# A graph layer with residual norm on one core: ScalarE issues the stores of the output and the loads of x_t, x and adj; SyncE's queue keeps the hops over HBM

## The reference: what is computed

```
u     = h h^T / sqrt(384);  p = softmax(u);  delta = p * adjacency
attn  = delta / (sum(delta over keys) + 1e-10)
ctx   = upper(attn) (h W_left^T + b_left) + diag(attn) (h W_self^T + b_self)
      + lower(attn) (h W_right^T + b_right)
o     = relu(layernorm(ctx, 1e-12) * gamma + beta)
out   = layernorm(h + o, 1e-5)
```

## Time and profile before

| | us |
|---|---|
| median of 3 runs | 458.61 |
| the profiled execution, whole | 459.64 |
| its span, first to last instruction | 457.9 |
| TensorE busy in it | 448.1 |
| VectorE busy | 386.6 |
| ScalarE busy | 323.9 |
| GpSimd busy | 209.6 |

### The profile page before, as it was taken

How to read it: one execution, slowest core, us unless ns; L and a number is a source line. 1 busy time by engine, 2 the same in 40 slices (tenths; PEclk the granted TensorE clock), 3 DMA queues, 4 the chain that set the end, 5 groups by cost and what they waited for, 6 DMA issues and landing times.

```text
span 457.9 us, 9725 instructions
## 1 busy us (share of the span) xinstructions
PE 448.1 (98%) x2636; PEld 445.3 (97%) x2636; DVE 386.6 (84%) x1366; ACT 323.9 (71%) x716; POOL 209.6 (46%) x295
## 2 busy tenths in 40 slices
PE   8999999999999999999999999999999999999993
PEld 7999999999999999999999999999999999998992
DVE  6877988888898887989878989888988888887876
ACT  6756677677678677678677678677677677676764
POOL 1144346553345553345554345553345553345542
PEclk9999999999999999999999999999999999999998
DMA  8765455666455565455566555566455666444312
GB/s 265 219 212 178 130 175 185 194 203 196 131 179 195 189 205 185 145 176 196 181 195 190 158 174 191 181 214 195 143 168 181 188 215 189 152 159 142 108 59 104
DMA packets 84227, 80.60 MB, mean 176 GB/s; under 512 B 7148, under 2 KB 76528, under 8 KB 84208
## 3 DMA queue, kind: packets, MB, share of 16 engines
q1 hardware_dynamic: 84000, 80.24, 55.0%
q10 hardware_dynamic: 144, 0.13, 0.1%
q0 software_dynamic: 64, 0.01, 0.0%
HBM read 52.04 MB, written 28.31 MB: 175 GB/s over the span
## 4 chain that ended last, share of the span: by engine, by line
PE 91%; DVE 2%; DMA 2%; ACT 1%; issue 1%; SPq 1%; POOL 1%; POOLq 0%; DVEq 0%; ACTq 0%
PE ps_proj L508 60%; PE ps_ctx L542 20%; PE ps_scores L485 3%; PE ps_scores L479 2%; PE ps_scores L481 2%; PE ps_proj L493 1%; PE ps_scores L431 1%; DMA cross_raw<-cross_dram 1%; DMA rows<-in_L_gnn_b_right 1%; PE ps_ctx L536 0%; ACT ps_scores L606 0%; SPq L332 0%; DVE delta L829 0%; POOL rstd L1138 0%; PE ps_ctx L538 0%
## 5 line engine op out<-in xcount | busy, mean ns | idle before, releaser
L508 PE MATMUL ps_proj<-w_hi,xt_split 128*128 128x384 f32 x1128 | 236.0, 334 | 0.0
L508 PEld LDWEIGHTS ps_proj<-w_hi,xt_split 128*128 128x128 f32 x1128 | 199.1, 188 | 0.0
L508 PE MATMUL ps_proj<-w_lo,xt_split 128*128 128x384 f32 x564 | 128.0, 334 | 0.0
L1138 POOL TENSOR_TENSOR rstd<-var_eps,minus_half 128x4 f32<-128x4 f32 x31 | 34.4, 1110 | 186.5 <-DVE var_eps L890 186.5
L508 PEld LDWEIGHTS ps_proj<-w_lo,xt_split 128*128 128x128 f32 x564 | 100.5, 188 | 0.0
L624 ACT ACTIVATE ps_proj<-bias 128x384 f32<-128x384 f32 x188 | 90.4, 494 | 2.0 <-DVE proj_lo L860 1.8
L1144 POOL TENSOR_TENSOR scaled<-normed,gamma_sb 128x384 f32<-128x384 f32 x60 | 61.7, 1029 | 30.9 <-ACT normed L654 30.9
L628 ACT ACTIVATE proj_hi<-ps_proj 128x384 fp32r<-128x384 f32 x128 | 63.4, 496 | 15.2 <-PE ps_proj L508 14.4
L648 ACT ACTIVATE ps_ctx<-ps_proj,diag 128x384 f32<-128x384 f32 x64 | 35.5, 555 | 49.2 <-PE ps_proj L508 49.2
L860 DVE TENSOR_TENSOR proj_lo<-ps_proj,proj_hi 128x384 fp32r<-128x384 f32 x128 | 67.3, 544 | 1.4 <-ACT proj_hi L628 1.4
L1148 POOL TENSOR_TENSOR shifted<-scaled,beta_sb 128x384 f32<-128x384 f32 x61 | 62.4, 1024 | 2.5
(11 more groups left out here) (113 smaller groups left out, 676.3 us busy)
## 6 DMA issues: line engine op xcount, KB each, us to landing
x_sb<-in_x SPq DMA_DIRECT2D x32, 384.0 KB, 4.3
xt_sb<-in_x_t SPq DMA_DIRECT2D x31, 384.0 KB, 3.8
out_dram<-out_sb SPq DMA_DIRECT2D x31, 384.0 KB, 2.9
adj_sb<-in_adj SPq DMA_DIRECT2D x32, 256.0 KB, 4.4
dt_dram<-turned SPq DMA_DIRECT2D x31, 256.0 KB, 2.0
dt_raw<-dt_dram SPq DMA_DIRECT2D x124, 64.0 KB, 2.0
cross_dram<-cross_turned SPq DMA_DIRECT2D x29, 256.0 KB, 2.0
cross_raw<-cross_dram SPq DMA_DIRECT2D x116, 64.0 KB, 2.0
```

The lines of the kernel that those rows point to most:

```text
L508: mm = nc.tensor.matmul(ps_proj[bank(at, g)][:, 0:H], halves[c][half], moving[w][:, c, :], start=False, stop=True, skip_group_check=True)
```

## The change

From the second batch on, SyncE's stream holds only the two hops. ScalarE's stream gets, in each batch b: the load of x_t of batch b + 4 behind the last `split_proj`, the load of x of batch b + 2 behind `split_xt`, the load of adj of batch b + 2 behind the last seed of the next batch, and behind it the store of the output of batch b - 2. So x_t is loaded for the batch b + 4 in place of b + 3, and the output is stored in the batch in which it is written and not in the one after. Each keeps a wait in front of it. The first batch's issues stay on SyncE, as do the last three output stores.

```
--- before.py
+++ after.py
-            def load(b, slot):
-                sp.dma_start(x_sb[slot][:], x_rows[b]).then_inc(x_loaded[slot], 16)
-                sp.dma_start(adj_sb[slot][:], adj_rows[b]).then_inc(adj_loaded[slot], 16)
...
             def one(at):
                 nxt, ahead, third = at.plus(1), at.plus(2), at.plus(3)
-                if at.plus(-3).exists(BATCHES):
-                    store(at.plus(-3))
-                if third.exists(BATCHES):
-                    if at.plus(-1).exists(BATCHES):
-                        sp.wait_ge(xt_lo_ready, at.n(1, C - 1))
+                if at.b == 0:
                     load_xt(third.n(1), third.slot(UNROLL))
-                if at.b == 0:
...
-                if ahead.exists(BATCHES):
-                    if at.plus(-2).exists(BATCHES):
-
-                        sp.wait_ge(y_ready, at.n(T, -T))
-                    load(ahead.n(1), ahead.slot(UNROLL))
                 if nxt.exists(BATCHES):
                     store_turned(nxt)
...
+            def store(at):
+                act.wait_ge(out_ready, at.n(T, T))
+                act.dma_start(out_rows[at.n(1)], out_sb[at.slot(2)][:]).then_inc(stored[at.slot(2)], 16)
+
+            def load_xt(at):
+
+                fourth = at.plus(4)
+                if fourth.exists(BATCHES):
+                    act.wait_ge(xt_lo_ready, at.n(1, C))
+                    act.dma_start(xt_sb[fourth.slot(UNROLL)][:], xt_rows[fourth.n(1)]).then_inc(xt_loaded[fourth.slot(UNROLL)], 16)
+
+            def load_x(at):
+                ahead = at.plus(2)
+                if ahead.exists(BATCHES):
+                    if at.plus(-2).exists(BATCHES):
+
+                        act.wait_ge(y_ready, at.n(T, -T))
+                    act.dma_start(x_sb[ahead.slot(UNROLL)][:], x_rows[ahead.n(1)]).then_inc(x_loaded[ahead.slot(UNROLL)], 16)
+
+            def load_adj(at):
+                ahead = at.plus(2)
+                if ahead.exists(BATCHES):
+
+                    act.wait_ge(delta_ready, at.n(T * T, 0))
+                    act.dma_start(adj_sb[ahead.slot(UNROLL)][:], adj_rows[ahead.n(1)]).then_inc(adj_loaded[ahead.slot(UNROLL)], 16)
...
@@ -700,6 +712,7 @@
                 if at.b == 0:
 
+                    load_xt(at)
                     return
...
                 split_proj(at, 3)
+                load_xt(at)
                 seed_ctx(at, 0)
...
                     split_xt(third)
+                load_x(at)
                 seed_ctx(at, 1)
...
                     seed_proj(nxt, 3)
+                load_adj(at)
+                if second.exists(BATCHES):
+                    store(second)
```

## The result

The changed kernel takes 498.86 us (median of 5 runs, 497.68 to 500.0) against 458.65 (458.46 to 460.08) for the kernel before, run beside it: a ratio of 1.0874, interval 1.0863 to 1.0886. It is 40 us slower. The forecast was 458.9 and no change; the range ended at 463.0. The profiled execution took 500.0 us with a span of 498.3, where before's took 459.64 with 457.9.

What follows compares the result with a forecast made beforehand. TensorE, gapless in 30 of 31 batches, was taken as the bound. Terms 0 + 0 + 0.3 = +0.3 us on the profiled 459.64 gave 459.9, in the median 458.9; the range was 457.4 to 463.0.

Steps and rivals of the forecast that it cites:

- What bounds the kernel, and that SyncE's time is worth nothing: TensorE runs without a gap in 30 of 31 batches, 13.71 us each; freeing SyncE shortens nothing.
- Part 1: Four more issues on ScalarE, 0.61 us each, 2.4 us a batch, fit its idle places; cost 0.
- the lower bound: ScalarE's issues cost nothing at all if each runs beside the activation before it; upper bound 1.46 us, the longest issue.
- Part 2: What moved transfers run beside: adj and output, issued amid the `cross_raw` loads, delay them within reserve; steady-batch cost 0.
- I count nothing: The load of x may hold up the store to `cross_dram`; the `dt_raw` loads stand before `cross_raw`, so 0 was counted.
- D: Added delay of `cross_raw` from bulk beside it: bounds 0 and 1.84 us, taken 0.5, against reserves of 0.44 and 1.18.
- Part 1's cover of `dt_full`: `dt_full` comes 0.2 us later in one batch, on average not; delay passes at most in full to L812 and `delta`.
- Part 2's rule weighed, taking turns: DMA engines alternate packets between loaded queues, so ScalarE's bulk takes every second turn beside the hop; no trace row showed it.
- the first rival: Scores' hop falls behind: `cross_raw` delay above 0.44 us accumulates until TensorE waits every batch; 461.6 or 464 us, chance 0.25.
- Part 3: The one late batch where TensorE waits 0.96 us, read as an instruction fetch; bounds -1.1 and +1.8, taken +0.3 us.
- the third rival: The late TensorE wait goes, as no x and adj loads queue behind the last `cross_raw`; 457.5 us, chance 0.15.
- The signs: Right: one TensorE wait near 415 us. Wrong: many for `delta` or a context seed, or none in the last turn.

Runs made afterwards that it cites:

- the 2 KB loads: Kernel before with four 2 KB loads into unread tiles added on ScalarE, at the changed kernel's four issue places; 459.28 us, ratio 1.0019.
- In a row, at another place: Kernel before with all four bulk transfers issued consecutively by ScalarE behind a batch's first `split_proj`, at before's time; 479.06 us, ratio 1.0444.
- the spread version: Kernel before with all four bulk transfers on ScalarE at about before's time, one at a time between activations; 459.13 us, ratio 1.0009.

## Why the prediction was wrong

- **What bounds the kernel, and that SyncE's time is worth nothing:** right. TensorE had no gap to give back.
- **Part 1, four issues at 0.61 us and a cost of 0:** the cost was right at these places (459.28 with the 2 KB loads), the reason only half. They take 0.38 to 0.41 us in the batch shown and run beside activations; the lower bound, nothing at all, was nearly the true one. In a row, at another place, they cost 20 us. Nothing in the sum went wrong here by its size.
- **Part 1, where the issues fall in time, and with it Part 2's "issued from about 217.5 to 218.5":** wrong, and the first step that failed. I put them at the place that their number in ScalarE's program has among the activations. The sequencer runs ahead: adj went out before two output activations and a seed that stand in front of it, 1.84 us before that seed's end at 221.66. It so fell at the store to `cross_dram`, 3.67 us ahead of the `cross_raw` loads (219.82 against 223.49), where the prediction had it behind their start; the output store, at 221.46, is 2.03 us ahead of them. The lead is not the whole of it. Before, the first output activation starts 1.17 us after the store to `cross_dram` (216.01 against 214.84); in the changed kernel 0.03 us after it, because the hop itself is late. So the delay, once there, brings the bulk closer to the hop, which the prediction did not see either. Held against `cross_raw`, it looked for the harm at the wrong hop.
- **Part 2, "I count nothing" for `cross_dram` and `dt_raw`:** the term of the sum that failed, put at 0. It was said of the load of x, and for it nearly true (x_t and x together: 0.9 us). For adj and the store no delay of these two hops was weighed at all. The D of the hop to `dt_full` is 1.56 us. The bounds of 0 and 1.84, which were made for `cross_raw`, hold it; the 0.5 taken there is a third of it. "Half of the engines are free" was read off the wrong hop's stretch, and off a before in which nothing shared it.
- **Part 1's cover of `dt_full`,** judged by one batch: a delay passes to L812 and `delta`, with 1.2 us to spare. But `dt_full` is in a loop whose reserve is 0.47 us. A reserve in one batch is used up once; against a delay that comes in every batch only the loop's counts.
- **Part 2's rule weighed, taking turns:** the trace now has the rows that it lacked. With both queues loaded 2.0 us became 3.3 for `dt_raw` and 3.5 for `cross_dram`, and the first rival's side of that weighing came.
- **Part 3, +0.3 us for the late wait:** can't be judged in the changed kernel, where it drowns. In the spread version that wait of TensorE is gone, and its profiled execution (458.58) is 1.06 below before's, as the third rival had it; its median is no better for it.
- **The rivals:** the first had the right mechanism, a lateness that adds up over the batches until TensorE waits each time. Its hop was wrong, and its price, "if VectorE makes most of it good and 0.1 remains", was a guess without a row: nobody makes it good, for every step of the loop waits for the one before. Of D less the reserve all remains, 1.1 to 1.4 us a batch. Worked out with D = 1.84 and a reserve of 0.44, this rival's own numbers would have given (1.84 - 0.44) x 27 - 1.18 = 36.6 us. The range stopped at 463.0 because of this one guess.
- **The signs:** a wait of TensorE for `delta` in many batches or for a seed of the context was to show me wrong. What came is a wait for the seed of a projection, 27 times, which none of the signs names, and beside it one of the weight loads for `delta`, 24 times.

## What to carry to other kernels

Before transfers are moved to another queue, draw the loops that run from batch to batch over a DMA, with the ties that come only from the order of an engine's stream, and work out each one's reserve as the batch's time less all steps of the loop; a delay larger than it costs the whole difference in every batch. Then place the moved transfers in time against each small hop of the loop, with the issue as early as its semaphores and the sequencer's lead allow, not where it stands among its engine's activations. Here the second queue freed only the issuing engine, and bulk that lay behind the hops in one queue lay beside them in two.

## What the runs showed of the hardware beyond this

- ScalarE issues a DMA in about 0.4 us (0.38 to 0.41 in the batch shown of the changed kernel) and goes on with activations beside it, but four issues in a row in front of a waiting activation stopped it for 1.51 us.
- Beside 256 and 384 KB on another queue, a 256 KB store to HBM took 3.5 us to land instead of 2.0, and 64 KB loads 3.3 instead of 2.0. Halving the bulk gives 2.8 and 3.0.
- With only the store moved, the same program took 458.5 to 460.5 us or 473.9 to 479.7, at the same granted clock. In the one long execution with a trace, an `rstd` on GpSimd that lasted 0.5 us longer stands just before the turn.
